# A metaformer network on one core: packed weight tails, transposes for folding sums, later gating and scatters in its expert layers

## What is computed

```
for each token x with its experts e and gates g:
    h = silu(x @ w1[e].T) * (x @ w3[e].T)        # 682 values
    y += g * (h @ w2[e].T)                       # 64 values
```

## Time and profile before

| | |
|---|---|
| median of 3 runs | 3013.59 us (3013.39 to 3016.9) |
| profiled execution, its own time | 3012.79 us |
| its span, first to last instruction | 3011.0 us |
| mean granted clock of PE | 0.783 |
| busy: PE, PEld, DVE, ACT, POOL | 1953.7, 1257.4, 1553.0, 1169.6, 831.9 us |
| dense up products (L577) of ffn0, of ffn1 | 146 to 431 us, 820 to 1106 us |
| sparse up products (L1099) of ffn2, of ffn3 | 1832 to 2226 us, 2573 to 2967 us |
| matmuls of the sparse up products (L1099) | 1872, 24 in each of 78 blocks |
| passes of the sparse fold (L1121), of the dense (L597) | 624 and 256, eight to a fold |

### The profile page before, as it was taken

How to read it: one execution, slowest core, us unless ns; L and a number is a source line. 1 busy time by engine, 2 the same in 40 slices (tenths; PEclk the granted TensorE clock), 3 DMA queues, 4 the chain that set the end, 5 groups by cost and what they waited for, 6 DMA issues and landing times. The chain is left out here.

```text
span 3011.0 us, 34082 instructions
## 1 busy us (share of the span) xinstructions
PE 1953.7 (65%) x9985; PEld 1257.4 (42%) x9985; DVE 1553.0 (52%) x2762; ACT 1169.6 (39%) x1971; POOL 831.9 (28%) x1010
## 2 busy tenths in 40 slices
PE   2599984887699974070100136999964542899994
PEld 1555542556555543070000124556534431556552
DVE  7733346433633346827689753444438173444543
ACT  4466651332466654243511213444423310344441
POOL 0311101000311110000000446775433154677542
PEclk8599996997599995555555557999986855899997
DMA  0000000000000000000000223444333631444433
GB/s 31 21 1 0 0 2 4 0 0 3 19 0 0 0 1 1 0 1 0 0 0 0 79 55 123 150 143 144 126 111 70 122 98 41 142 146 147 139 127 125
DMA packets 201900, 163.55 MB, mean 54 GB/s; under 512 B 157612, under 2 KB 173228, under 8 KB 201516
## 3 DMA queue, kind: packets, MB, share of 16 engines
q1 hardware_dynamic: 183596, 141.29, 16.3%
q0 software_dynamic: 18176, 20.75, 2.1%
HBM read 77.67 MB, written 29.82 MB: 36 GB/s over the span
## 5 line engine op out<-in xcount | busy, mean ns | idle before, releaser
L1192 DVE TENSOR_TENSOR ffn_hidden<-ffn_silu,ffn_up_ps 114x512 f32<-114x512 f32 x468 | 321.3, 686 | 405.0 <-ACT ffn_silu L1159 394.4
L1099 PE MATMUL ffn_up_ps<-ffn_turned,ffn_up_now 128*114 128x512 f32 x1872 | 515.5, 411 | 4.7 <-DVE ffn_turned L1181 3.0
L1159 ACT ACTIVATE ffn_silu<-ffn_up_ps 114x512 f32<-114x512 f32 x468 | 281.1, 601 | 443.1 <-PE ffn_up_ps L1099 442.7
L1099 PEld LDWEIGHTS ffn_up_ps<-ffn_turned,ffn_up_now 128*114 128x114 f32 x1872 | 309.5, 178 | 174.0 <-issue 62.3
L1052 POOL DMA_INDIRECT results<-ffn_yout,ffn_dest x312 | 300.4, 963 | 267.1 <-DVE ffn_yout L1174 188.7
L637 ACT ACTIVATE ffn_hidden<-ffn_up_ps,ffn_b 128x512 f32<-128x512 f32 x512 | 310.4, 697 | 0.0
L761 POOL DMA_INDIRECT slots<-ffn_rows,ffn_slot x256 | 245.6, 959 | 154.6 <-issue 84.3
L588 PE MATMUL ffn_y_ps<-ffn_hidden,ffn_down 128*64 128x512 f32 x1024 | 247.5, 605 | 0.0
L652 POOL COPY ffn_spread<-ffn_G 128x512 f32 (+1 forms) x128 | 78.3, 616 | 537.9 <-PE ffn_gate_ps L566 458.9
L1111 PE MATMUL ffn_y_ps<-ffn_hidden,ffn_down 114*64 114x512 f32 (+1 forms) x936 | 218.2, 601 | 0.0
L196 PE MATMUL ffn_turn_ps<-ident,ffn_parts 128*128 128x128 f32 x256 | 66.2, 429 | 230.2 <-DVE ffn_parts L157 229.9
(11 more groups left out here) (391 smaller groups left out, 3474.2 us busy)
## 6 DMA issues: line engine op xcount, KB each, us to landing
ffn_up_now<-ffn_up SPq DMA_DIRECT2D x78, 682.0 KB, 3.4
ffn_down<-in_ffn_w SPq DMA_DIRECT2D x78, 192.0 KB
ffn_xin<-slots SPq DMA_DIRECT2D x78, 160.0 KB
ffn_stage<-in_ffn_w SPq DMA_DIRECT2D x64, 170.5 KB, 3.0
ffn_xin<-slots SPq DMA_DIRECT2D x78, 128.0 KB
ffn_both<-results SPq DMA_DIRECT2D x16, 512.0 KB, 6.8
sht_mix<-in_sht_weights SPq DMA_DIRECT2D x8, 1024.0 KB, 7.8
results<-ffn_yout,ffn_dest POOLq DMA_INDIRECT x312
```

Of the source, the lines that this page charges most:

```text
L1099: last = nc.tensor.matmul(up_ps[w][n % 2][0:sizes[c], :], up[:, g % 2, w, c * size:c * size + sizes[c]], turned[:, g % 2, part, :], start= ...
L1159: nc.scalar.activation(silu[0:sizes[c], n % 2, :], up_ps[0][n % 2][0:sizes[c], :], ACT.Silu)\
L1192: nc.vector.tensor_tensor(hidden[0:sizes[c], g % 2, c, :], silu[0:sizes[c], n % 2, :], up_ps[1][n % 2][0:sizes[c], :], ALU.mult).then_inc( ...
```

## The change

Dense mixtures: `turn_back` no longer multiplies with `k.fold`. It transposes `total` into all 512 columns of `out_ps`; DVE adds the two halves to `k.X` one after the other, the second waiting for the first.

Sparse mixtures:

- The 682 units are cut into five chunks of 128 and a tail of 42 (`CHUNKS`, `TAIL`). The tails of `w1` and `w3` lie in one stationary operand of 106 columns: 42, a gap of zeros up to 64, and 42. One pair of passes makes both. Silu reads partitions 0 to 41 and writes 64 to 105, where the linear part lies. The tail's `hidden` chunk is zeroed once, and its down product runs over all 128 partitions.
- The tail is the third chunk in the order: 0, 1, tail, 2, 3, 4.
- `fold_back` becomes `turn_back`, four transposes by `k.ident`. `take_y` gates both halves (128x512, into `y_gated`) and then adds them. It now stands after the third chunk, for block g-2 instead of g-1.
- ACT copies `total` right after the turned rows, ahead of the silu of the fourth chunk.
- POOL scatters results of blocks up to g-3, single issues counted: three per block while it still stores rows, up to six after that. `yout` has 9 buffers for 3, the copies of gates and destinations 13 for 4.
- The up weights are laid out in DRAM in two pieces of 693 columns per expert; they were 682 each.

```diff
@@ -594,8 +594,8 @@
                     if not first:
                         pe.wait_ge(x_added, g)
                     for t in range(GROUP):
-                        last = nc.tensor.matmul(out_ps[:, t * CH:(t + 1) * CH], total[:, t * P:(t + 1) * P],
-                                                k.fold[:, :], start=True, stop=True)
+                        last = nc.tensor.transpose(out_ps[:, t * P:(t + 1) * P], total[:, t * P:(t + 1) * P],
+                                                   k.ident[:, :])
                     last.then_inc(turned_back, 1)
...
@@ -677,8 +677,10 @@
                 def add(g):
                     dve.wait_ge(turned_back, g + 1)
                     x = k.X[:, bass.ds(g * GROUP, GROUP), :]
-                    nc.vector.tensor_tensor(x, out_ps[:, 0:GROUP * CH].rearrange("p (t c) -> p t c", c=CH), x,
-                                            ALU.add).then_inc(x_added, 1)
+                    both = out_ps[:, :].rearrange("p (t a c) -> p t a c", a=2, c=CH)
+                    nc.vector.tensor_tensor(x, both[:, :, 0, :], x, ALU.add).then_inc(even_added, 1)
+                    dve.wait_ge(even_added, g + 1)
+                    nc.vector.tensor_tensor(x, both[:, :, 1, :], x, ALU.add).then_inc(x_added, 1)
...
@@ -707,6 +709,10 @@
 TOKENS = TILES * P
+CHUNKS = HID_B // P
+TAIL = HID_B - CHUNKS * P
+UP_COLS = 2 * CHUNKS * P + CH + TAIL
+UP_PIECE = UP_COLS // 2
...
@@ -733,9 +739,8 @@
 def sparse_stage(nc, sem, k, name):
-    chunks = -(-HID_B // P)
-    size = -(-HID_B // chunks)
-    sizes = [min(size, HID_B - c * size) for c in range(chunks)]
+    chunks = CHUNKS + 1
+    order = [0, 1, CHUNKS] + list(range(2, CHUNKS))
...
+        up_parts = sb("up", [P, E, 2, UP_PIECE], F32R)
...
+            loads = [(e, piece) for e in range(E) for piece in (0, 1)]
...
-            XR, AR, YR, READ = 3, 4, 3, 8
+            XR, AR, YR, READ = 3, 13, 9, 8
...
+            yout, y_gated = sbi("yout", [P, YR, GROUP, CH]), sbi("y_gated", [P, GROUP, P])
...
-                def scatter(g):
-                    pool.wait_ge(y_ready, g + 1)
-                    for q in range(GROUP):
-                        nc.gpsimd.indirect_dma_start(k.results, bass.IndirectOffsetOnAxis(dest[:, g % AR, q:q + 1], 0),
-                                                     yout[:, g % YR, q, :], None).then_inc(y_stored[g % YR], 16)
-
+                def scatter(n):
+                    g, q = n // GROUP, n % GROUP
+                    if q == 0:
+                        pool.wait_ge(y_ready, g + 1)
+                    nc.gpsimd.indirect_dma_start(k.results, bass.IndirectOffsetOnAxis(dest[:, g % AR, q:q + 1], 0),
+                                                 yout[:, g % YR, q, :], None).then_inc(y_stored[g % YR], 16)
+
+                scattered = 0
                 for g in range(SLOT_BLOCKS):
...
-                    if g >= 2:
-                        scatter(g - 2)
-                scatter(SLOT_BLOCKS - 2)
-                scatter(SLOT_BLOCKS - 1)
+                    at_once = GROUP - 1 if FIRST_PAIRS + g < TILES // 2 else GROUP + 2
+                    for n in range(scattered, min(scattered + at_once, GROUP * max(g - 2, 0))):
+                        scatter(n)
+                        scattered += 1
+                for n in range(scattered, GROUP * SLOT_BLOCKS):
+                    scatter(n)
...
-                def up_product(g, c):
-                    n = chunks * g + c
-                    if c == 0:
+                def up_product(g, i):
+                    c, n = order[i], chunks * g + i
+                    if i == 0:
                         pe.wait_ge(up_loaded[g % 2], 16 * (g // 2 + 1))
                         pe.wait_ge(hi_copied, g + 1)
                         pe.wait_ge(lo_set, g + 1)
                     if n >= 2:
                         pe.wait_ge(hidden_done, n - 1)
                     for w in (0, 1):
-                        for part in (0, 1):
-                            last = nc.tensor.matmul(up_ps[w][n % 2][0:sizes[c], :],
-                                                    up[:, g % 2, w, c * size:c * size + sizes[c]],
-                                                    turned[:, g % 2, part, :], start=(part == 0), stop=(part == 1))
-                        last.then_inc(up_done, 1)
+                        first, cols = ((w * CHUNKS + c) * P, P) if c < CHUNKS else (2 * CHUNKS * P, CH + TAIL)
+                        if c < CHUNKS or w == 0:
+                            for part in (0, 1):
+                                last = nc.tensor.matmul(up_ps[w][n % 2][0:cols, :], up[:, g % 2, first:first + cols],
+                                                        turned[:, g % 2, part, :], start=(part == 0), stop=(part == 1))
+                            last.then_inc(up_done, 1 if c < CHUNKS else 2)
                 def down_product(g):
+
                     pe.wait_ge(down_loaded[g % 2], 16 * (g // 2 + 1))
                     if g >= 1:
                         pe.wait_ge(total_copied, g)
-                    for c in range(chunks):
-                        pe.wait_ge(hidden_done, chunks * g + c + 1)
-                        half = c % 2 * CH
-                        last = nc.tensor.matmul(y_ps[half:half + CH, :],
-                                                down[0:sizes[c], g % 2, c, :],
-                                                hidden[0:sizes[c], g % 2, c, :], start=(c < 2), stop=(c >= chunks - 2))
+                    else:
+                        pe.wait_ge(tails_zeroed, 1)
+                    for i, c in enumerate(order):
+                        pe.wait_ge(hidden_done, chunks * g + i + 1)
+                        half = i % 2 * CH
+                        last = nc.tensor.matmul(y_ps[half:half + CH, :], down[:, g % 2, c, :], hidden[:, g % 2, c, :],
+                                                start=(i < 2), stop=(i >= chunks - 2))
                     last.then_inc(down_done, 1)
-                def fold_back(g):
+                def turn_back(g):
                     pe.wait_ge(total_copied, g + 1)
                     if g >= 1:
                         pe.wait_ge(y_ready, g)
                     for q in range(GROUP):
-                        last = nc.tensor.matmul(out_ps[:, q * CH:(q + 1) * CH], total[:, q * P:(q + 1) * P],
-                                                k.fold[:, :], start=True, stop=True)
-                    last.then_inc(folded, 1)
+                        last = nc.tensor.transpose(out_ps[:, q * P:(q + 1) * P], total[:, q * P:(q + 1) * P],
+                                                   k.ident[:, :])
+                    last.then_inc(turned_back, 1)
...
-                        nc.scalar.activation(silu[0:sizes[c], n % 2, :], up_ps[0][n % 2][0:sizes[c], :], ACT.Silu)\
+                        source, to = (slice(0, P),) * 2 if c < CHUNKS else (slice(0, TAIL), slice(CH, CH + TAIL))
+                        nc.scalar.activation(silu[to, n % 2, :], up_ps[0][n % 2][source, :], ACT.Silu)\
                             .then_inc(silu_done, 1)
-                        if c == 2 and g + 1 < SLOT_BLOCKS:
+                        if i == 2 and g + 1 < SLOT_BLOCKS:
                             copy_x(g + 1)
-                        if c == 3 and g >= 1:
+                        if i == 2 and g >= 1:
                             copy_total(g - 1)
                 copy_total(SLOT_BLOCKS - 1)
...
-                    dve.wait_ge(folded, g + 1)
+                    dve.wait_ge(turned_back, g + 1)
                     dve.wait_ge(aux_set, 2 * (g + 1))
                     if g >= YR:
                         dve.wait_ge(y_stored[g % YR], 16 * GROUP * (g // YR))
-                    nc.vector.tensor_tensor(yout[:, g % YR, :, :],
-                                            out_ps[:, 0:GROUP * CH].rearrange("p (q c) -> p q c", c=CH),
-                                            gate[:, g % AR, :].unsqueeze(2).to_broadcast([P, GROUP, CH]), ALU.mult)\
+                    nc.vector.tensor_tensor(y_gated[:, :, :], out_ps[:, :].rearrange("p (q c) -> p q c", c=P),
+                                            gate[:, g % AR, :].unsqueeze(2).to_broadcast([P, GROUP, P]), ALU.mult)\
+                        .then_inc(halves_gated, 1)
+                    dve.wait_ge(halves_gated, g + 1)
+                    nc.vector.tensor_tensor(yout[:, g % YR, :, :], y_gated[:, :, 0:CH], y_gated[:, :, CH:P], ALU.add)\
                         .then_inc(y_ready, 1)
...
+                nc.vector.memset(hidden[:, :, CHUNKS, :], 0.0).then_inc(tails_zeroed, 1)
+                dve.wait_ge(tails_zeroed, 1)
                 set_low(0)
                 for g in range(SLOT_BLOCKS):
-                    for c in range(chunks):
-                        n = chunks * g + c
+                    for i, c in enumerate(order):
+                        n = chunks * g + i
                         dve.wait_ge(silu_done, n + 1)
```

(13 more changed lines are left out.)

65 lines of the change are left out of this document (32 added, 33 removed).

## The result

| | before | after |
|---|---|---|
| median of 4 runs each, side by side | 3015.24 us (3013.39 to 3017.41) | 2946.81 us (2938.43 to 2949.66) |
| profiled execution, its span | 3012.79, 3011.0 us | 2949.41, 2947.6 us |
| mean granted clock of PE | 0.783 | 0.772 |

The ratio is 0.9768, with an interval of 0.9745 to 0.9791: 68 us less, where 82.5 were forecast. The direction was right, 2946.81 lies in the range of 2907 to 2952, and the forecast of 2931.0 was 16 us too low.

What follows compares the result with a forecast made beforehand. PE's sequence alone was taken to bound the changed loops. The terms summed to -36 - 38 - 13 (dense loops) + 3 + 1.5 = -82.5 us, from 3012.79 to 2930.3, or 2931 as a median; range 2907 to 2952.

Steps and rivals of the forecast that it cites:

- term 1: Sparse loops, PE: 22 up matmuls per block for 24, at 0.23 us each over 78 blocks; 36 us saved.
- Rival B: Sparse loops: the longer weight load shows in full on 20 matmuls a block, 19 us, giving 2950; chance 0.06.
- term 2: Sparse loops, PE: eight fold passes become four transposes, 0.50 us in each of 76 blocks; 38 us saved.
- term 3: Sparse loops: PE's wait at the third chunk after the fold stays; nothing, bounds -23 to +15 us.
- rival A: Sparse loops: the third-chunk wait goes (2908), or a new one comes behind the transposes (2946); chance 0.14, split evenly.
- term 4: Sparse loops, DVE: the doubled gating, 1.1 to 1.64 us, fits beside the down products; nothing.
- term 5: Sparse loops, ACT: copying `total` (0.58 us) ahead of the first silu after the down products just fits; taken as 0.
- term 6: Sparse loops, first 23 blocks: POOL with three scatters takes 9.04 us, just under PE's 9.15; nothing.
- Rival D: Sparse loops: POOL or the x loads pace the loop, at most 11 us, giving 2942; chance 0.05.
- term 7: Sparse loops: x loads come late at blocks 8, 16, 24 and 32; +1.4 us a loop, +3 us.
- term 8: End of the sparse loops: the last two blocks' scatters follow a gating 0.7 us longer; +1.5 us for both loops.
- rival C: Sparse loops: transposes make PE's clock fall, 7 us more a block; 3204 if in half the blocks; chance 0.03.

Runs made afterwards that it cites:

- both_early: Changed kernel with the next block's x turned after the first chunk instead of the second, and x loaded ahead of the down weights; 2917.58 us, ratio 0.9672.
- gate_late: Changed kernel with the two gating instructions moved back behind the sixth chunk; 2963.57 us, ratio 0.9832.
- x_sooner: Changed kernel with SP loading x of block g+1 ahead of block g's down weights, PE's order kept; 2934.68 us, ratio 0.9737.

## Why the prediction was right in its direction and 16 us off

By stages (start to start, two traces of each kernel averaged), the dense mixtures lost 12.7 us and the sparse ones 61.4, together 74. The stages without an edit took 4 us longer, 1095 for 1091. These were 1089 to 1098 in the traces of all kernels, with no order by what was edited, so I take them as chance; that none of it belongs to the change isn't shown.

The mechanism held: PE's sequence set the pace in the changed loops, and but for single waits for x nothing else took it over. What the sum had at the wrong size are the steady block (4 us), the end of the sparse stages behind the last scatter (2 us), the loads of x (1 to 2 us) and the start of the sparse loops (about 1 us).

- **Two up matmuls fewer** (term 1, 36 us): right. Undone alone it costs 0.45 us a block and 32 us. That width costs nothing was nearly right; it costs 2 to 3 us, at restarts. Rival B's mechanism exists, at about a seventh of its price.
- **Fold to transposes** (term 2, 38 us): right, 0.45 to 0.51 us for 0.50. Undone alone: 31 us.
- **The third chunk's wait** (term 3): stayed, as forecast, and no second one came. Neither half of rival A happened, though both_early shows that its 0.27 us were there to be had.
- **Gating** (term 4): nothing, and gate_late shows that its cover is worth 19 us. My figure of up to 1.1 us a block without the cover was four times too high.
- **Copy of `total`** (term 5): no wait for it shows in the rows, but no run undid it alone.
- **POOL** (term 6): the arithmetic held. With eight issues it bounds the loop at 10.3; with seven it runs level with PE. Rival D did not come true.
- **Loads of x** (term 7, 3 us): too small, by a wrong reading. I gave every load the 3.76 us of one block of before and let only the distance shrink. For fourteen of the sixteen loads above that was near enough; the two that took 5.25 and 5.46 us made their blocks 1.7 and 1.9 us longer, one in each trace, and that is the 1 to 2 us by which the term was short. x_sooner prices all waits for x at 5 to 6 us. Why single loads are longer isn't settled; the down weights, issued 1.7 us ahead, and POOL's stores are candidates, and neither was taken away alone.
- **The steady block**: 9.20 for 9.15, in 72 blocks 4 us, of which the width is most.
- **First two distances of turns in each loop**. No fold and one tail chunk lie in them, so the sum had 0.46 us for each loop. They were 13.5 us together before and 13.7 after, averages of four loops that lie up to 1.3 us apart. That is about 1 us less gain in both loops, not more than those lie apart.
- **Dense loops**: 13 us forecast, 13 measured.
- **The tail** (term 8, 1.5 us): behind the last turn of x lie two blocks' worth of terms 1 and 2, so a gain of 2 x 0.96 - 0.7 = 1.2 us a loop was forecast. Up to the last scatter it came: 27.1 us for 28.2. But from there to SP's load of the results 12.0 us pass, for 10.9 before, in both loops and in both traces of each kernel. No term had that. It takes 2 us off the gain, and no run tells why.
- **The clock** (rival C): 1.00 in both stretches of the loops, as before. The rule of the Trainium skill (TensorE: Matmul & The Clock Gate, Part 4: PE-mode transpose), by which the full clock does not engage for transposes, does not hold for transposes set between matmuls as here: eight in each 9.2 us cost nothing of it.

The 8 us missing in the sparse stages are thus 4 from the block, 1 or 2 more of waits for x than forecast, 2 behind the last scatter and about 1 at the start of the loops. Of the rest of the 16 us, 4 are the stages without an edit, and 2 the trace that the sum was made against, which lay that much under the median; the last 2 are within the spread of the runs (2938 to 2950 us).

## What to carry to other kernels

Count a saving at the places where its instructions stand, and look at the ends of a loop by themselves: what follows the last block can take back what the last block gained. When the pacing engine gets faster, give a load with slack under a microsecond the longest time that a trace shows for it and not the usual one. A wait between two buffers is a place to put other work, but only when that work's input is already there: move the load first, then the work.

## What was not expected of the hardware

- A weight load that is 12 ns longer (190 against 178 ns) leaves the 0.23 us spacing of matmuls alone and shows only where PE starts anew, some 30 ns for three restarts a block.
- Loads of x of one size, in one kernel, were turned 3.54 to 3.99 us after their issue in fourteen cases and 5.25 and 5.46 us after it in two.
- In the lightly loaded spherical stage the granted clock of the same program was 0.93 over 40 us in one execution and 0.65 in another, and the stage 156.1 and 159.9 us long.
- Instructions of DVE can start up to 0.1 us before the recorded end of the one ahead (2108.86 + 0.43 = 2109.29 in gate_late, and the hidden product starts at 2109.20), so a sum of lengths can overstate a busy stretch.
